# A layer pair for 16 sequences: 36 keep-warm products in place of 2 around TensorE's last pause

## What is computed

```python
# second layer, for every sequence: state s is 32 heads x 8 x 8
def step(s, rkvw):
    r_t, k_t, v_t, w_t = rkvw
    a = k_t[:, :, :, None] * v_t[:, :, None, :]
    out = jnp.einsum('bhk,bhkd->bhd', r_t, u * a + s)      # the state is read with r
    return (a + w_t[:, :, :, None] * s, out)
...
att = group_norm(att) * gn_w + gn_b
x = x + att * g @ Wo.T
xn2 = _ln(x); sx2 = _token_shift(xn2)
xk = xn2 + sx2 * ffn_maa_k
xr = xn2 + sx2 * ffn_maa_r
rr = jax.nn.sigmoid(xr @ ffn_Wr.T)
kk = jnp.square(jax.nn.relu(xk @ ffn_Wk.T))
x = x + rr * (kk @ ffn_Wv.T)
```

## Time and profile before

| | us |
|---|---|
| median of 3 runs | 678.86 |
| the three runs | 680.0, 678.82, 678.86 |
| the profiled execution | 680.22 |
| its span (first to last instruction) | 678.40 |
| PE busy in the span | 638.5 (94%) |
| mean granted TensorE clock | 0.992 |

### The profile page before, as it was taken

The page is one execution under the profiler, slowest core; times in us unless marked ns, Lnnn a source line. Parts: engine busy times, 40 slices in busy tenths (PEclk is TensorE's granted clock), DMA queues, the critical chain, the costliest instruction groups (busy, mean ns, idle before and its releaser), DMA issues. The chain is left out here.

```text
span 678.4 us, 17274 instructions
## 1 busy us (share of the span) xinstructions
PE 638.5 (94%) x5865; PEld 554.2 (82%) x5865; DVE 604.6 (89%) x1430; ACT 575.2 (85%) x2073; POOL 312.9 (46%) x440
## 2 busy tenths in 40 slices
PE   6889999999999999999999999999999989989777
PEld 4767787898888888988988888888888878768656
DVE  3699689999999999999999999999999997887774
ACT  1688999899999999999999998999999998765542
POOL 1245362645563554636464645546364644352220
PEclk9999999999999999999999999999999998999989
DMA  9920040220404050403223050504022230500000
GB/s 354 289 74 10 2 129 13 82 61 17 125 8 135 1 142 1 134 9 90 60 64 86 11 139 3 148 1 136 14 85 65 64 86 12 161 1 9 9 1 16
DMA packets 51133, 48.34 MB, mean 71 GB/s; under 512 B 5998, under 2 KB 46822, under 8 KB 50662
## 3 DMA queue, kind: packets, MB, share of 16 engines
q1 hardware_dynamic: 51046, 47.24, 24.0%
HBM read 28.62 MB, written 3.93 MB: 48 GB/s over the span
## 5 line engine op out<-in xcount | busy, mean ns | idle before, releaser
L1535 ACT ACTIVATE SC<-SC,NMX 128x128 f32<-128x128 f32 x512 | 200.4, 403 | 0.2
L1535 ACT ACTIVATION_READ_ACCUMULATOR SC<-SC,NMX 128x1 f32 x512 | 103.7, 203 | 0.0
L886 PE MATMUL PS_T<-CST,SC 128*128 128x128 f32 x512 | 80.7, 280 | 7.0 <-ACT SC L1535 3.1
L1217 DVE TENSOR_REDUCE NMX<-SC 128x4 f32<-128x512 f32 x128 | 84.8, 671 | 1.5 <-POOL SC L1751 0.9
L1545 ACT ACTIVATE PT<-PS_T 128x512 f32<-128x512 f32 x120 | 71.1, 593 | 11.7 <-PE PS_T L886 11.0
L886 PEld LDWEIGHTS PS_T<-CST,SC 128*128 128x128 f32 x512 | 56.6, 141 | 25.0 <-ACT PT L1545 11.0
L1300 DVE TENSOR_TENSOR_SCAN SS<-W,AJ 128x1024 f32<-128x1024 f32 x32 | 73.1, 2284 | 0.1
L784 PE MATMUL PS_B<-MX,W 128*128 128x128 f32 x504 | 62.9, 275 | 0.9 <-DVE MX L1270 0.9
L1749 POOL TENSOR_TENSOR SC<-SC,MADD 128x512 f32<-128x512 f32 x48 | 60.3, 1283 | 7.3 <-DVE SC L1197 7.2
L784 PE MATMUL PS_B<-B_LT,W 128*128 128x128 f32 x512 | 61.4, 278 | 1.3 <-ACT B_LT L1473 1.2
L784 PEld LDWEIGHTS PS_B<-B_LT,W 128*128 128x128 f32 x512 | 58.4, 192 | 3.9 <-ACT B_LT L1473 3.2
(11 more groups left out here) (235 smaller groups left out, 1630.8 us busy)
## 6 DMA issues: line engine op xcount, KB each, us to landing
W<-EW SPq DMA_DIRECT2D x28, 512.0 KB, 4.1
V<-values_by_head SPq DMA_DIRECT2D x28, 512.0 KB, 5.7
W<-in_weights SPq DMA_DIRECT2D x1, 4160.0 KB, 17.8
ENC<-in_enc SPq DMA_DIRECT2D x16, 128.0 KB, 2.3
out<-X SPq DMA_DIRECT2D x16, 128.0 KB, 1.9
values_by_head<-VC SPq DMA_DIRECT2D x14, 128.0 KB, 1.8
X<-in_x SPq DMA_DIRECT2D x1, 1664.0 KB, 22.2
W<-in_weights SPq DMA_DIRECT2D x1, 1280.0 KB, 8.4
```

The source lines that it names most:

```text
L886: last = pe.transpose(PS_T[:, j * T:(j + 1) * T], SC[:, nr(b, a) % 2, g, j, :], ident)
L1217: dve.tensor_reduce(NMX[:, nr(b, a) % 2, GH * g:GH * g + GH], SC[:, nr(b, a) % 2, g], AX_X, ALU.max, negate=True)\
L1535: last = act.activation(SC[:, nr(b, a) % 2, g, j, :], SC[:, nr(b, a) % 2, g, j, :], ACT.Exp, bias=NMX[:, nr(b, a) % 2, h:h + 1], accum_out ...
```

## The change

The table `KEEP_WARM` gets other numbers for two pieces of the last sequence: 8 products in place of 2 ahead of `d_own(15)`, and 28 in place of none ahead of `d_read(15)`. Nothing else is changed.

```diff
-    ('d_keyrec', 0, 14): 0, ('d_own', 0, 15): 2, ('d_read', 0, 15): 0,
+    ('d_keyrec', 0, 14): 0, ('d_own', 0, 15): 8, ('d_read', 0, 15): 28,
```

## The result

The changed kernel takes 683.85 us in the median of 4 runs (683.1 to 684.73), against 678.84 us before (4 runs, 677.33 to 680.0): the ratio is 1.0072, 95% interval 1.0055 to 1.0088. It is slower by 5.0 us. The forecast was 685.0 us, range 682.8 to 686.9.

The account below looks back on a forecast made before the run. Bound by the closing chain through TensorE's state read of sequence 15: 680.22 us profiled, + 4.37 queue, + 1.70 half clock, - 0.87 and - 0.29 gained back, is 685.1; adjusted to the median 685.0 us, range 682.8 to 686.9.

Parts of the forecast that it names:

- The chain and the place: End of the kernel: VectorE's chain passes to TensorE at sequence 15's state read; the 28 products stand in the short pause before it.
- Six products ahead of d_own(15), + 0.25 us of delay for XK: TensorE's long pause: six more products take 1.34 us and start XK 0.25 us later, bounds 0 and 0.45.
- 28 products, 6.25 us, of which 2.1 us fit the gap: Ahead of d_read(15): nine products fit the gap, the other 19 lie on the path; the state read waits 4.37 us longer.
- The clock, + 1.7 us: Behind the long pause TensorE's clock still falls to half for 3.4 us, costing 1.7 us of queue.
- Gained back, 0.87 and 0.29 us: Behind the 28: state read at full clock saves 0.87 us, its way to the transpose's end 0.29 us.
- The sum: Whole kernel: + 4.37 + 1.70 - 0.87 - 0.29 = + 4.91 on the profiled 680.22 us, so 685.1 us.
- To the median: Whole kernel: half of a 0.2 us remainder above the median comes off the sum, giving 685.0 us, 6.1 us slower.
- The two levels of before: Kernel before: runs at 678.8 us lose little to the clock's fall, those at 680 do; its terms make 1.16 us.
- the first rival: Behind the long pause the clock keeps full level, or its fall lies within the pause: 683.3 us; chance 0.27.
- The rival on the other side: Ahead of d_read(15): a product costs one record, 0.112 us and not 0.223, so not slower, 680.06 us; chance 0.03.

Follow-up runs that it names:

- pause 14 / read 9: 14 keep-warm products ahead of d_keyrec(14, 0), in the long pause, and 9 ahead of d_read(15), against the kernel before: 678.29 us, ratio 0.9986.
- pause 14: Only 14 products added ahead of d_keyrec(14, 0), in the long pause, against the kernel before; run twice: 678.58 us (ratio 0.9997) and 678.11 us (0.9986).
- pause 14 / read 28: 14 products ahead of d_keyrec(14, 0), in the long pause, and 28 ahead of d_read(15), against the kernel before: 683.21 us, ratio 1.0054.
- read 28 again: Second run of the kernel with only the 28 products ahead of d_read(15) added to the kernel before: 684.51 us, ratio 1.0069.
- own 8 / read 14: 8 products in place of 2 ahead of d_own(15) and 14 in place of none ahead of d_read(15), against the kernel before: 680.91 us, ratio 1.0014.
- own 2: Kernels that keep 2 products ahead of d_own(15), as the kernel before does: 678.84 us for the kernel before.
- own 8: 8 products in place of 2 ahead of d_own(15); as a run, only this changed against the kernel before: 678.50 us, ratio 1.0006.
- read 28: Only 28 products in place of none ahead of d_read(15), against the kernel before, first run: 684.83 us, ratio 1.0090.
- read 9: Only 9 products in place of none ahead of d_read(15), against the kernel before: 679.44 us, ratio 1.0013.
- changed again: The changed kernel (8 products ahead of d_own(15), 28 ahead of d_read(15)) measured once more against the kernel before: 684.14 us, ratio 1.0075.

## Why the prediction was right, step by step

- **The chain and the place.** Right. The chain goes over to TensorE at XK, VectorE waits for the transpose, and the 28 alone give the loss.
- **Six products ahead of d_own(15), + 0.25 us of delay for XK.** The effect was named rightly, the size was not: it is 0, the lower bound. The products are 1.34 us (x16 records in 1.95 us against x4 in 0.61), and SM started 5.34 us behind the first AJ (652.59 - 647.25) in place of 4.00 (651.48 - 647.48), but it took 0.61 us and not 1.47. XK starts 6.38 us behind the first AJ (653.63 - 647.25), and 6.37 before.
- **28 products, 6.25 us, of which 2.1 us fit the gap.** Right to the hundredth in the chain (6.25 us). pause 14 / read 9 against pause 14 shows that nine fit, and pause 14 / read 28 that the rest cost 4.2 us.
- **The clock, + 1.7 us.** Right in the profile of the changed kernel: half for 3.4 us, which costs 1.66 us.
- **Gained back, 0.87 and 0.29 us.** Right. From the start of the state read to the end of the span it was 678.4 - 658.50 = 19.9 us before, and 682.9 - 664.14 = 18.8 after: 1.1 us.
- **The sum**, 4.91 us over the profiled execution's 680.22, was 685.1 us against 684.73. Of the 0.4 us, 0.25 is the delay of XK that didn't come, and 0.2 is that the whole stretch started 0.23 us earlier (647.25 for 647.48).
- **To the median.** Here the forecast is 1.15 us too high (685.0 against 683.85). The step that failed is to take the profiled execution's clock for the median's. I corrected the side of before for it (678.8 and not 680.22), but charged the changed kernel the full 1.7 us, and the profiled execution is the slowest of its four. Its mean granted clock is 0.993, that of the three others 0.995, 0.995 and 0.997: they had less half clock, though the record does not say whether in this stretch or ahead of it. What pause 14 / read 28 costs with the clock up in its profile, 683.21 in the median, is close to the first rival's 683.3; the measured median lies between this rival and the forecast.
- **The two levels of before**, 678.8 and 680, as without and with a fall. Only half confirmed. The half clock costs 1.1 us of the stretch. But the 29 runs of before lie between 677.5 and 680.4 without a gap, and the first AJ of sequence 15 started anywhere between 645.15 and 649.58 us in the profiles, so most of the spread comes from ahead of this stretch. The profiles show where part of it arises. Each has one or two more stretches of 3.4 us at half clock between 558 and 636 us, where all these kernels have the same program. From VectorE's instruction of line 1409 near 548 us to the same one near 645 us it is 95.6 us in the two profiles of pause 14 (one fall, at 594) and 98.1 us in four others with two falls, near 559 and 631 (changed, read 28 again, pause 14 / read 28, pause 14 / read 9). That the falls make this difference is likely, but not shown. Another 2 us of the spread stood already near 548 us, where that instruction started at 547.2 to 549.6; its cause stays open.
- **The rival on the other side**, one record a product, is out: 28 products are x56 records, and a product costs 0.223 us, over the 0.166 us at which this rival would have won.

The Trainium skill's page "TensorE: Matmul & The Clock Gate" (section "Why this matters for your kernels") advises to avoid long idle gaps between bursts. By the profiles this holds where the products stand in the gap: all four with 14 products in the long pause kept 1.00 behind it. Shortening the pause to 2.71 us was not enough: the clock fell at its end, or within 0.4 us behind it, in three of the four profiles with that pause (both of the changed kernel, own 8 / read 14).

Here the products cost more than the fall. The fall cost 1.1 us in the stretch of before; the change paid 5.9 us of later start of the state read for 1.1 us on its other side, and didn't avoid the fall.

## What to carry to other kernels

In this kernel keep-warm work kept the clock up only ahead of the instruction that waits longest, in TensorE's order; put behind it, it was plain queue for the next instruction, and could pay the half clock too. Even at the right place its gain here, 1.1 us of 679 in the stretch, is not told from nothing in the medians. Before adding such products, read three numbers in the profile: the idle time just ahead of the instruction they stand before, the price of one, and what the fall costs on the chain; here 2.1 us at full clock, 0.223 us and 1.1 us, so nine were free while the clock was up, and 28 were not. Where executions vary by more than the effect, measure from a fixed instruction near the change to the end.

## What the runs showed of the hardware

The same GpSimd instruction, SM (line 1781, 128x256), took 1.47 us when it started alongside VectorE's product of SS with KR (line 1306), and 0.61 us when it started 1.3 us later, alongside AJ (line 1291), which reads PSUM. The changed kernel, timeline of VectorE and GpSimd there:

```profile
651.03 1.22 DVE L1306 TENSOR_TENSOR SS<-SS,KR 128x1024 f32<-128x1024 f32 x1
...
652.17 1.21 DVE L1291 TENSOR_TENSOR AJ<-PS_S,KR 128x1016 f32<-128x1016 f32 x1
652.59 0.61 POOL L1781 TENSOR_TENSOR SM<-XM 128x256 f32<-128x256 f32 x1 [4.73 <-ACT XM L1473]
```

In the kernel before, line 1306 ran when SM started (651.48 to 652.95):

```profile
651.25 1.22 DVE L1306 TENSOR_TENSOR SS<-SS,KR 128x1024 f32<-128x1024 f32 x1
```

It was so in all twelve profiles: 1.47 to 1.48 us with own 2, 0.61 us with own 8. The other sequences of the kernel before fit in. SM took 1.06 us at 145.87 and 0.90 us at 220.66, where VectorE's product of line 1316 (SS with KR) still ran for 0.60 and 0.43 us, and 1.03 us at 593.19, where the scan of line 1300 still ran for 0.63 us. Where such an instruction had 0.2 us or less left, SM took 0.61 to 0.64 us. Alongside line 1127, which reads X, also in SBUF, it took 0.61 us (at 258.55, for example). So it is not enough that both engines read SBUF. The VectorE instructions beside which SM was long read two tiles of SBUF, those beside which it ran in full at 0.61 us at most one; that this is the cause is an argument, not shown.

The clock's fall is not tied to a fixed length of the pause: with 4.05 us it came 0.9 us ahead of XK's product (read 28), just at it (read 28 again, read 9) or 0.7 us behind it (before), with 2.71 us at it (changed), 0.4 us behind it (changed again) or only 5.5 us later (own 8). In this stretch it then stood for 3.4 us, or for about 6.8 us (before and read 28).
